# Phase stage of a layered kernel: the position weights go onto the triangle of the running sums, and VectorE forms both products and both half sums of a block

## The reference

```python
z = conv(x @ W_mem)                       # width 4, causal
k_val, s_raw = z[..., :256].reshape(b, l, K, H), z[..., 256:]
q_re, q_im = x @ W_q                      # 4 groups of heads share a query
p_w = exp(clip(score_scale * s_raw, -20, 20) + log_w)     # (b, l, K)
phi = k_val[..., None] * theta
merged = concat([p_w, p_w * cos(phi), p_w * sin(phi)])
den, num_re, num_im = split(cumsum(merged, axis=1))
state_re, state_im = num_re / max(den, 1e-4), num_im / max(den, 1e-4)
out_re = sum_m(state_re * q_re + state_im * q_im)
out_im = sum_m(state_im * q_re - state_re * q_im)
y = out_re @ W_re + out_im @ W_im
y = y_val * silu(y_gate)
x += y @ W_out
```

## Time and profile before

| what | us |
|---|---|
| median of 3 runs | 449.14 |
| lowest, highest | 446.56, 449.43 |
| the profiled execution | 445.03 |
| its span, first to last instruction | 443.2 |
| granted clock of TensorE, mean over the span | 0.981 of full speed |

### The profile page before, as it was taken

The page is one execution under the profiler, slowest core; times in us unless marked ns, Lnnn a source line. Parts: engine busy times, 40 slices in busy tenths (PEclk is TensorE's granted clock), DMA queues, the critical chain, the costliest instruction groups (busy, mean ns, idle before and its releaser), DMA issues.

```text
span 443.2 us, 14132 instructions
## 1 busy us (share of the span) xinstructions
PE 400.4 (90%) x5937; PEld 337.3 (76%) x5937; DVE 311.5 (70%) x695; ACT 251.0 (57%) x496; POOL 220.9 (50%) x269
## 2 busy tenths in 40 slices
PE   7979999999999998789979968789689897999997
PEld 4656677777677776689969856668688887889996
DVE  6788989988888774668788976665898957322221
ACT  2557878888888889765535424412723045444541
POOL 2458657756666761345543702310499643544440
PEclk8989999999999999999989989999899999999999
DMA  4186642523211102800000160340000061000000
GB/s 151 26 303 211 230 135 82 192 86 91 81 38 33 36 4 98 309 2 1 1 1 1 36 291 0 139 190 0 0 3 1 1 258 75 1 0 2 0 2 24
DMA packets 10543, 34.77 MB, mean 78 GB/s; under 512 B 2160, under 2 KB 7280, under 8 KB 8688
## 3 DMA queue, kind: packets, MB, share of 16 engines
q1 hardware_dynamic: 10192, 33.08, 21.4%
...
HBM read 33.60 MB, written 0.26 MB: 76 GB/s over the span
## 4 chain that ended last, share of the span: by engine, by line
PE 60%; DVE 20%; POOL 10%; ACT 5%; issue 4%; DMA 1%; SPq 0%; DVEq 0%; POOLq 0%; ACTq 0%
PE ps L1582 10%; PE ps L1537 8%; PE ps L1074 8%; PE ps L1060 6%; PE ps L1569 4%; PE ps L394 3%; PE ps L1552 3%; PE ps L455 2%; POOL sb_arena L983 2%; PE ps L380 2%; PE ps L745 2%; POOL sb_mid L997 2%; PE ps L340 2%; ACT sb_arena L1503 1%; DVE sb_mid L896 1%
## 5 line engine op out<-in xcount | busy, mean ns | idle before, releaser
L1503 ACT ACTIVATE sb_arena<-ps 128x1024 f32<-128x1024 f32 x128 | 123.4, 1019 | 22.1 <-PE ps L1569 22.0
L1582 PE MATMUL ps<-sb_arena 128*25 128x128 f32 (+1 forms) x2048 | 69.5, 275 | 0.6 <-issue 0.3
L1582 PEld LDWEIGHTS ps<-sb_arena 128*25 128x25 f32 (+1 forms) x2048 | 50.6, 97 | 8.4 <-issue 1.3
L1537 PE MATMUL ps<-sb_halves 128*128 128x512 f32 x192 | 54.6, 420 | 1.7 <-DVE sb_arena L1325 1.0
L1104 POOL TENSOR_TENSOR sb_halves<-sb_big,sb_halves 128x704 fp32r<-128x704 f32 x20 | 33.7, 1688 | 38.8 <-ACT sb_halves L1098 38.8
L484 POOL TENSOR_TENSOR sb_halves<-sb_big,sb_halves 128x256 fp32r<-128x256 f32 x32 | 23.7, 761 | 46.7 <-ACT sb_halves L468 46.7
L1170 DVE SCALAR_TENSOR_TENSOR sb_arena<-ps,sb_w_q,sb_arena 128x176 f32<-128x176 f32 x40 | 15.9, 401 | 42.7 <-ACT sb_arena L1122 42.5
L1537 PEld LDWEIGHTS ps<-sb_halves 128*128 128x128 f32 x192 | 34.6, 193 | 14.6 <-issue 6.2
L1074 PE MATMUL ps<-sb_halves 128*128 128x352 f32 x240 | 42.9, 332 | 2.0 <-POOL sb_halves L1104 2.0
L1397 POOL TENSOR_TENSOR sb_big<-sb_arena 128x256 f32<-128x256 f32 x31 | 19.0, 613 | 49.4 <-DVE sb_arena L1286 49.4
L1074 PEld LDWEIGHTS ps<-sb_halves 128*128 128x128 f32 x240 | 39.1, 189 | 3.3 <-DVE sb_arena L1170 1.7
...
## 6 DMA issues: line engine op xcount, KB each, us to landing
sb_big<-in_w_gu SPq DMA_DIRECT2D x2, 3520.0 KB, 11.4
...
```

What stands on the lines that cost most here:

```text
L1503: nc.scalar.activation(probs[:, n % P_SLOTS].rearrange("p a g n -> p a (g n)"), ps[:, bank:bank + 2], ACT.Exp, scale=XD ** -0.5).then_inc( ...
L1537: i = T.matmul(ps[:, 7], ctx_half[:, t % 2, c, kt], wkv_half[:, d, kt], start=(n + kt == 0), stop=(n == 2 and kt == KT - 1))
L1582: i = T.matmul(ps[32 * gg:32 * gg + m, 6, j * P:(j + 1) * P], v_sb[:, t % V_SLOTS, 4 * gg + j, head], probs[:, n % P_SLOTS, a, gg], start= ...
```

## The change

The position weights no longer go onto the waves. They go onto the triangle: for block `j`, batch `b` and head `u` of the two in a block, `tri_w` is `tri` with each row (position) multiplied by `pw[:, b, 2j + u]`. Since the two heads of a block have different weights, the running sums of a block are eight matmuls with 64 columns of `cs` as weights instead of four with 128, each head into its half of the PSUM partitions. GpSimd makes the triangles (four tensor_scalar instructions of 128 x 128 a block, 60 in all), VectorE those of block 0. `weigh` and L882 go.

VectorE forms both products of a block in one instruction of 1024 elements: the PSUM bank is read twice, and the queries lie as -q_im, q_re, q_im, so that two overlapping windows of 512 are the two factors. ACT writes them in two instructions a group. One further VectorE instruction of 512 elements makes both half sums; GpSimd adds nothing any more, and TensorE takes two products a batch in every group (4 matmuls a block where the first half had 6).

Further: the fraction of group 0 is made batch by batch, that of batch 0 while VectorE waits for the second projection; the clamp and reciprocal of the denominators move behind block 2; the first `turn_y` moves in front of the last two products, and the copies of `y` move forward; `tri_w` lies where the second half of `w_gu` for experts 4 to 15 will be, so SyncE loads that part (2.16 MB) only when the last running sum is made, ahead of `w_down`, and ACT waits for it before it converts those experts.

The diff, cut to its core:

```diff
@@ sync
-            for k in range(KT):
-                if k:
-                    sp.wait_ge(sem("h_projected"), HT_FFN)
-                sp.dma_start(w_gu[:, k], io["w_gu"][k]).then_inc(sem("gu_loaded"), 16)
+            sp.dma_start(w_gu[:, 0], io["w_gu"][0]).then_inc(sem("gu_loaded"), 16)
+            sp.wait_ge(sem("h_projected"), HT_FFN)
+            for n in (slice(0, LATE_GU.start), slice(LATE_GU.stop, UNITS * 2 * EI)):
+                sp.dma_start(w_gu[:, 1, n], io["w_gu"][1][:, n]).then_inc(sem("gu_loaded"), 16)
+
+            sp.wait_ge(sem("state_ready"), FT)
+            sp.dma_start(w_gu[:, 1, LATE_GU], io["w_gu"][1][:, LATE_GU]).then_inc(sem("late_gu_loaded"), 16)
@@ tiles
+        qf = [cut(6144 + 768 * kq, 768) for kq in range(4)]
+        def query_pairs(kq):
+            a = qf[kq]
+            return bass.AP(tensor=a.tensor, offset=a.offset, ap=[a.ap[0], [256, 2], [1, 512]])
@@ tensor_phase
-                    if kq:
-                        pe.wait_ge(sem("re_weighted"), kq)
-                    else:
-                        pe.wait_ge(sem("first_re_weighted"), 1)
-                    pe.wait_ge(sem("im_weighted"), kq + 1)
-                    if j >= 2:
-                        pe.wait_ge(sem("state_used"), 2 * (j - 1))
                     for c in range(2):
                         for b in range(B):
-                            i = T.matmul(ps[:, 1 + j % 2, (c * B + b) * P:(c * B + b + 1) * P],
-                                         cs[:, kq % 2, c, b, jj * P:(jj + 1) * P], tri[:], start=True, stop=True)
+                            for u in range(2):
+                                rows = slice(64 * u, 64 * u + 64)
+                                i = T.matmul(ps[rows, 1 + j % 2, (c * B + b) * P:(c * B + b + 1) * P],
+                                             cs[:, kq % 2, c, b, jj * P + 64 * u:jj * P + 64 * u + 64],
+                                             tri_w[:, kq % 2, jj, b, u], start=True, stop=True)
...
+                if j == FT - 1:
+                    pe.wait_ge(sem("y_gated"), 2 * B)
+                    turn_y(0)
@@ vector_phase
+                    step(dve, nearest(0, 0))
+                    step(dve, fraction(0, 0))
...
+            dve.wait_ge(sem("pw_ready"), 1)
+            for b in range(B):
+                for u in range(2):
+                    i = V.tensor_scalar(tri_w[:, 0, 0, b, u], tri[:], pw[:, b, u:u + 1], None, ALU.mult)
+            i.then_inc(sem("first_tri_weighed"), 1)
...
-                for c in range(2):
-                    V.tensor_tensor(pa[:, j % 3, c], ps[:, 1 + j % 2].rearrange("p (c n) -> p c n", c=2),
-                                    qf[kq][:, 2 * c:2 * c + 2], ALU.mult).then_inc(sem("state_used"), 1)
-                if kq >= 2:
-                    dve.wait_ge(sem("state_used"), 2 * j + 2)
-                    V.tensor_tensor(pa[:, j % 3, 1, 0], pa[:, j % 3, 1, 0], pa[:, j % 3, 1, 1], ALU.add
-                                    ).then_inc(sem("out_im"), 1)
+                V.tensor_tensor(pa[:, j % 3].rearrange("p c h n -> p c (h n)"),
+                                ps[:, 1 + j % 2][:, None, :].to_broadcast([P, 2, 512]), query_pairs(kq), ALU.mult
+                                ).then_inc(sem("state_used"), 1)
+                dve.wait_ge(sem("state_used"), j + 1)
+                V.tensor_tensor(pa[:, j % 3, :, 0], pa[:, j % 3, :, 0], pa[:, j % 3, :, 1], ALU.add
+                                ).then_inc(sem("out_summed"), 1)
@@ pool_phase
+            def weigh_tri(j):
+                kq, jj = j // 4, j % 4
+                if kq >= 2:
+                    pool.wait_ge(sem("state_ready"), j - 7)
+                for b in range(B):
+                    for u in range(2):
+                        i = G.tensor_scalar(tri_w[:, kq % 2, jj, b, u], tri[:], pw[:, b, 2 * j + u:2 * j + u + 1], None,
+                                            ALU.mult)
+                i.then_inc(sem("tri_weighed"), 1)
...
             for j in range(FT):
                 kq, jj = j // 4, j % 4
-                pool.wait_ge(sem("state_used"), 2 * j + 1)
-                G.tensor_tensor(pa[:, j % 3, 0, 0], pa[:, j % 3, 0, 0], pa[:, j % 3, 0, 1], ALU.add
-                                ).then_inc(sem("out_re"), 1)
...
-                if jj == 0 and kq < 3:
-                    weigh(kq + 1, 1, "sin_ready", "im_weighted")
-                if jj == 1 and kq < 3:
-                    weigh(kq + 1, 0, "cos_ready", "re_weighted")
+                if j + 4 < FT:
+                    weigh_tri(j + 4)
```

137 lines of the change are left out of this document (69 added, 68 removed).

## The result

The changed kernel takes 451.46 us (median of 7 runs, 450.03 to 453.22) against 446.56 for the kernel before (7 runs, 442.76 to 449.43, the three of the forecast among them). The ratio is 1.0117, with a 95% interval of 1.0073 to 1.0161: it is slower, by about 5 us. The forecast was 1.5 us faster. The 451.46 lies inside the forecast's range of 443.5 to 452.6 by luck: that range was laid around the median of the first three runs of the kernel before (449.14), and laid around the median of all seven it would be 440.9 to 450.0. The direction was wrong.

What follows compares the result with a forecast made beforehand. No single engine bound the stage: TensorE, VectorE and GpSimd were each near 90% in its loop, after a late start. Start -3.4, loop +1.5, tail 0, clock 0.4 back: -1.5 us, giving 447.6; 8-in-10 range 443.5 to 452.6.

Steps and rivals of the forecast that it cites:

- I take 0.34 for 128 elements, between 0.23 and 0.59, nearest to the cast.: GpSimd's price in us for one tensor_scalar triangle; floor half a 256-element cast (0.45), ceiling a two-input instruction of 192 elements.
- from about 0.5: Price in us of one GpSimd triangle from which GpSimd stops hiding behind the block loop and sets its end.
- GpSimd's sum: Sixty triangles at 0.34 (20.4 us), two fractions and six gates: some 28 us in the 46 to 352, so GpSimd hides.
- The second rival: GpSimd becomes the bound: triangles at 0.588 each, 35.3 us, plus 7 of waits; loop ends 3.7 later, 452.8 us; chance 0.13.
- The start: Before the block loop: first product moves from 316.54 to 313.1, 3.4 us gained, VectorE and TensorE meeting there.
- the first: Rival: port locks cost little or nothing against one-input GpSimd instructions, product nears 1.16; -4.3 us, or 444.8; chance 0.17.
- VectorE's loop: Block loop with VectorE as bound: 37.1 us own work plus 1.8 waiting for GpSimd, 38.9 against 37.4 before.
- TensorE: Per block in the loop: running sums 0.9 to 1.1 us with halves side by side, 2.0 to 2.1 in all, hidden.
- The 0.4 us that the forecast took back for the clock: Loss charged because TensorE idles more between blocks of the loop and its clock may drop to 1.2 GHz.
- The tail: After the loop, to the last output sums: 0 to 0.2 us gained, counted as 0; late expert weights charged nothing.
- The rule on the shared port: VectorE, in two-port mode or with two SBUF inputs, and GpSimd share ports held per instruction; 1.8 us of loop waits charged.
- the third rival: Full exclusion at the port VectorE and GpSimd share, nothing outside the lock: 3.9 us on the forecast, 451.5; chance 0.12.

## Why the prediction was wrong

**The step that failed: "I take 0.34 for 128 elements, between 0.23 and 0.59, nearest to the cast."** It measured 0.597 at the least, just above the upper bound, and 0.766 with the waits. The cast, also with one SBUF input, was a bad neighbour: a tensor_scalar with a weight per partition costs 0.27 us and 2.5 ns a column on GpSimd, the cast of 256 columns 0.45 with its waits. By bounds of 0.23 and 0.59 the value could be 0.34 or 0.59, and the forecast said itself where it decides, "from about 0.5". The runs agree with that threshold: at 0.434 and 0.392 GpSimd hides, at 0.597 it doesn't. With so near a threshold inside the bounds, a chance of 0.13 for the rival was too low.

**GpSimd's sum.** "Some 28 us in the 46" became 44.9 for the triangles alone, with the fractions 4.7 more, where the window of 46 us became 51.1; from 308.04 to the last triangle at 359.11 it never rested. Each triangle also waited 0.17 us on average (0.766 - 0.597), which the forecast had charged to VectorE's account only. In the run with tensor_tensor of 128 it is 0.16 (0.551 - 0.392) and with half the columns 0.17 (0.609 - 0.434), so these waits came on top of each price.

**The second rival** was the mechanism. Its 35.3 us and its 7 us of waits are 42.3, measured 44.9. It put the end of the loop 3.7 us later than before; measured from the same exponentials it is 7.0 (54.77 - 47.76). The missing 3.3 us are GpSimd's too: the rival had the last triangle ready 48.2 us after the first could start, and it was 51.1 (2.6 more for the triangles with their waits, 0.4 for two gates that took 1.6 instead of 1.2); the rest is 0.4 at the last block. The rival's 452.8 us were 3.7 above the base used then; by medians the loss is 4.9.

**The start** was right: forecast 6.9 after the exponentials (313.1), measured 6.80. One part of it was wrong and cost nothing. It charged VectorE 1.0 for twelve meetings with a triangle; the ten instructions from the rounding at 308.29 to the fraction at 312.39 took 5.74 us together in the changed kernel and 5.54 in the run without triangles, so 0.2 in all. TensorE sets the start; the same step had VectorE and TensorE meet there. Of the rivals the first had the lock against a one-input GpSimd instruction right.

**VectorE's loop**: 38.9 forecast, 38.83 without triangles and 39.28 with 36 of them, where the forecast meant 60 that hide. With 60 that do hide it is 40.17 (tensor_tensor) and 40.68 (half the columns). So the term was 1.3 to 1.8 low, inside the range that it was given. The product was 1.22 as taken; one part that was low is the fractions' holds, 1.88 and 1.44 for sums of 0.69 in the run without triangles, so 1.9 us for both where 0.3 to 0.6 was put.

**TensorE** was right: 1.02 us for a block's running sums (0.9 to 1.1 forecast), no drain to be seen in the pitch of 2.08. The 0.4 us that the forecast took back for the clock came out as nothing in the changed kernel: the gap ahead of the loop went and others came, as it said, but behind GpSimd's queue they were hidden. The rule of the Trainium skill that spoke against it, TensorEngine Tiling (Array Packing), section Tiling Modes, that a change of mode drains TensorE, is borne out at most by the 1.2 us that the loop of the kernel before lost with halves, 0.08 a block. **The tail** gained 0.35 (0 to 0.2 forecast), and no DMA was waited for.

**The rule on the shared port** stands in the Trainium skill, SBUF — State Buffer, section SBUF: two separate sides (the prediction gave another section of that page). The runs bear it out for GpSimd's two-input instructions: 1.08 for 0.28 us on VectorE's triangles behind multiplies of 1.04. For a one-input GpSimd instruction they don't, and the measurement decides: behind a tensor_scalar of 0.6 us or more VectorE's roundings take 0.48 and 0.69, where they take 0.43 and 0.69 without triangles. Full exclusion, the third rival, would have shown there.

With the one term put right (0.39 as tensor_tensor), the change is near what the forecast said (1.5 us faster): 0.9 us faster by medians, a difference that this measurement can't tell from none.
